# A four-layer graph network in split precision: products with high parts ahead of those with low parts at four waits, and the last output tile in two halves of columns

## What is computed

```
L0: attention over edges with 8 heads, Wo, layer norm,
    relu(h1 @ W1 + b1) @ W2 + b2 with 1024 hidden features, layer norm
L1: h @ wc + mean over edges of (h @ wn) + bias
L2: gates = softmax(h @ gate_W + gate_b), the best 2 of 4 experts;
    each expert twice: relu(mean_over_edges(h) @ Wl + bl + h @ Wr)
L3: H = X @ W + b, summed over edges and self loops with
    rsqrt(deg[src]) * rsqrt(deg[dst]), then relu
```

## Time and profile before

| | |
|---|---|
| median of 3 runs | 472.1 us (471.57 to 472.28) |
| the profiled execution, its own time | 472.32 us |
| its span in the trace | 470.3 us |
| TensorE's granted clock over the span | 0.996 of full speed |
| busy: TensorE products | 450.2 us, 96% |
| busy: TensorE weight loads (beside products) | 326.7 us, 69% |
| busy: VectorE, ScalarE, GpSimd | 310.4, 191.0 and 150.0 us |
| HBM read and written | 36.07 and 1.05 MB |

### The profile page before, as it was taken

The page is one execution under the profiler, slowest core; times in us unless marked ns, Lnnn a source line. Parts: engine busy times, 40 slices in busy tenths (PEclk is TensorE's granted clock), DMA queues, the critical chain, the costliest instruction groups (busy, mean ns, idle before and its releaser), DMA issues.

```text
span 470.3 us, 5919 instructions
## 1 busy us (share of the span) xinstructions
PE 450.2 (96%) x2096; PEld 326.7 (69%) x2096; DVE 310.4 (66%) x569; ACT 191.0 (41%) x266; POOL 150.0 (32%) x101
## 2 busy tenths in 40 slices
PE   8999999989899999799999999999999999999996
PEld 3456544434358888578778788888888888888765
DVE  5999868999997998953865836252263237134864
ACT  5898834537123440352632262133303332227230
POOL 4000033212112954454243444044434444344100
PEclk9999999989999999999999999999999999999999
DMA  8770007500000656145020222223221332020002
GB/s 275 160 294 1 1 2 168 101 0 0 1 1 1 149 144 200 24 79 191 1 64 27 91 89 91 89 89 113 90 91 32 115 144 77 14 89 1 0 1 89
DMA packets 24058, 37.48 MB, mean 80 GB/s; under 512 B 5728, under 2 KB 5984, under 8 KB 24032
## 3 DMA queue, kind: packets, MB, share of 16 engines
q1 hardware_dynamic: 21584, 32.80, 20.7%
q0 software_dynamic: 2160, 4.19, 5.2%
q10 hardware_dynamic: 288, 0.13, 0.1%
HBM read 36.07 MB, written 1.05 MB: 79 GB/s over the span
## 4 chain that ended last, share of the span: by engine, by line
PE 72%; DVE 16%; issue 5%; ACT 3%; POOL 2%; DVEq 1%; DMA 1%; POOLq 0%
PE ps L1240 16%; PE ps L1242 15%; PE ps L1241 15%; PE ps L1302 4%; PE ps L1313 4%; PE ps L1269 3%; PE ps L1268 3%; PE ps L1390 2%; DVE stats L762 2%; PE ps L1295 2%; DVE rsum L955 2%; DVE e_sb L395 1%; DVE one_src L836 1%; PE ps L1386 1%; PE ps L1412 1%
## 5 line engine op out<-in xcount | busy, mean ns | idle before, releaser
L473 POOL TENSOR_TENSOR w_lo<-w_stage,w_hi 128x1024 fp32r<-128x1024 f32 x21 | 51.6, 2456 | 136.4 <-ACT w_hi L559 125.7
L559 ACT ACTIVATE w_hi<-w_stage 128x2048 fp32r<-128x2048 f32 x22 | 42.0, 1909 | 53.4 <-PE ps L1242 53.4
L474 POOL TENSOR_TENSOR w_lo<-w_stage,w_hi 128x1024 fp32r<-128x1024 f32 x21 | 55.2, 2628 | 0.0
L1240 PE MATMUL ps<-w_hi,hid_hi 128*128 128x512 f32 x128 | 49.9, 390 | 0.5 <-DVE hid_lo L1151 0.5
L1242 PE MATMUL ps<-w_hi,hid_lo 128*128 128x512 f32 x128 | 49.8, 389 | 0.0
L1241 PE MATMUL ps<-w_lo,hid_hi 128*128 128x512 f32 x128 | 49.8, 389 | 0.0
L1240 PE MATMUL ps<-T_hi,w_hi 128*128 128x512 f32 (+1 forms) x112 | 41.0, 366 | 0.4 <-POOL w_lo L474 0.4
L1241 PE MATMUL ps<-T_lo,w_hi 128*128 128x512 f32 (+1 forms) x112 | 40.2, 359 | 0.0
L1242 PE MATMUL ps<-T_hi,w_lo 128*128 128x512 f32 (+1 forms) x112 | 40.2, 359 | 0.0
L1149 DVE TENSOR_SCALAR tmp<-ps,bl 128x512 f32<-128x512 f32 x16 | 12.0, 750 | 39.9 <-ACT hid_hi L713 39.9
L497 POOL TENSOR_TENSOR rstd<-vareps,scalars 128x1 f32<-128x1 f32 x24 | 15.9, 664 | 62.6 <-DVE vareps L764 62.6
(11 more groups left out here) (227 smaller groups left out, 984.4 us busy)
## 6 DMA issues: line engine op xcount, KB each, us to landing
w_stage<-in_L_gnn_Wr SPq DMA_DIRECT2D x8, 1024.0 KB, 5.3
w_stage<-in_L_gnn_Wl SPq DMA_DIRECT2D x8, 1024.0 KB, 5.0
w_stage<-in_L_gnn_W SPq DMA_DIRECT2D x5, 1024.0 KB, 5.7
x_sb<-in_x SPq DMA_DIRECT2D x4, 256.0 KB, 3.7
w_q<-in_L_gnn_Wq SPq DMA_DIRECT2D x1, 1024.0 KB, 7.8
w_k<-in_L_gnn_Wk SPq DMA_DIRECT2D x1, 1024.0 KB, 10.1
w_v<-in_L_gnn_Wv SPq DMA_DIRECT2D x1, 1024.0 KB, 5.7
w_o<-in_L_gnn_Wo SPq DMA_DIRECT2D x1, 1024.0 KB, 11.2
```

The lines of the kernel that those rows point to most:

```text
L473: gp.tensor_tensor(w_lo[h][:, 0:2], stage[s][:, 0:2], f32(w_hi[h][:, 0:2]), ALU.subtract)
L474: gp.tensor_tensor(w_lo[h][:, 2:4], stage[s][:, 2:4], f32(w_hi[h][:, 2:4]), ALU.subtract)\
L559: nc.scalar.activation(w_hi[home(u)][:], stage[u % 2][:], ACT.Copy).then_inc(hi_made, 1)
L1240: nc.tensor.matmul(goal, a_hi, b_hi, start=start, stop=False, **kw)
```

## The change

Five edits.

1. W1's second half: for its first bank, all eight products with high weights come first, after a wait for the high part alone (`hi_made`); then comes the wait for the low part and the four products with it.
2. Layer L2's mix over edges: in each step `k` the four products with `R4_hi` come first, after a wait for `hr_hi_made`, then the wait for `hr_lo_made` and the four with `R4_lo`.
3. Each expert's second layer: for `k` = 0 the eight products with `hid_hi` come first (after `hid_hi_made`), then the four with `hid_lo`. Other `k` are as before.
4. The last layer's mix: in steps 1 to 3 the four products with `R_hi` come ahead of the four with `R_lo`. On VectorE the low part of tile 1 is made ahead of `norm_shift` for tile 3.
5. The last output tile is computed in two halves of 256 columns. The left half stays in bank 7, the right half goes to bank 0. Each half has its own 12 products, its own two passes on VectorE and its own store. The start with `j` = 0 now covers three tiles only. Twelve products of 512 columns become 24 of 256.

```
+        def last_bank(t, half):
+            return 0 if half == 1 else 4 + t
...
-            for t in range(NT):
+            for t in range(NT - 1):
                 sp.wait_ge(x4_made, t + 1)
                 sp.dma_start(out[t * P:(t + 1) * P, :], x_sb[:, t, :]).then_inc(stored, 16)
-            sp.wait_ge(stored, 16 * NT)
+            for half in range(2):
+                sp.wait_ge(x4_made, NT + half)
+                cols = slice(half * HN, (half + 1) * HN)
+                sp.dma_start(out[(NT - 1) * P:NT * P, cols], x_sb[:, NT - 1, cols]).then_inc(stored, 16)
+            sp.wait_ge(stored, 16 * (NT + 1))
...
-            norm_shift(LN5, NT - 1)
-            for t in range(WHOLE, NT):
+            def last_row_lo(t):
                 v.wait_ge(last_hi_made, t - WHOLE + 1)
                 nc.vector.tensor_tensor(R_lo[:, t, :], h_sb[:, t, :], f32(R_hi[:, t, :]), ALU.subtract)\
                   .then_inc(last_lo_made, 1)
+            last_row_lo(WHOLE)
+            norm_shift(LN5, NT - 1)
+            for t in range(WHOLE + 1, NT):
+                last_row_lo(t)
...
+            def finish(n, t, cols=slice(0, D), half=None):
+                v.wait_ge(last_done, n)
+                v.wait_ge(bias_row_made, t + 1)
+                nc.vector.scalar_tensor_tensor(tmp[:, t, cols], ps[:, last_bank(t, half), cols], isd[:, t:t + 1],
+                                               tmp[:, t, cols], ALU.mult, ALU.add).then_inc(last_sum, 1)
+                v.wait_ge(last_sum, n)
+                v.wait_ge(nan_added, t + 1)
+                nc.vector.scalar_tensor_tensor(x_sb[:, t, cols], tmp[:, t, cols], 0.0, x_sb[:, t, cols], ALU.max,
+                                               ALU.add).then_inc(x4_made, 1)
...
+            for t in range(NT - 1):
+                finish(t + 1, t)
+            for half in range(2):
+                finish(NT + half, NT - 1, slice(half * HN, (half + 1) * HN), half)
...
-            hi, lo = weights(W1B)
-            for j in range(DT, FT):
+            hi, lo = w_hi[home(W1B)], w_lo[home(W1B)]
+            pe.wait_ge(hi_made, W1B + 1)
+            for k in range(DT):
+                nc.tensor.matmul(ps[:, DT, :], hi[:, k, col(0)], T_hi[:, k, :], start=k == 0, stop=False)
+                nc.tensor.matmul(ps[:, DT, :], hi[:, k, col(0)], T_lo[:, k, :], start=False, stop=False)
+            pe.wait_ge(lo_made, W1B + 1)
+            for k in range(DT):
+                last = nc.tensor.matmul(ps[:, DT, :], lo[:, k, col(0)], T_hi[:, k, :], start=False, stop=k == DT - 1)
+            last.then_inc(ff_done, 1)
+            for j in range(DT + 1, FT):
...
+                pe.wait_ge(hr_hi_made, k + 1)
+                for j in range(DT):
+                    nc.tensor.matmul(ps[:, 4 + j, :], R4_hi[:, k, col(j)], c_hi[:, k, :], start=k == 0, stop=False)
                 pe.wait_ge(hr_lo_made, k + 1)
                 for j in range(DT):
-                    goal = ps[:, 4 + j, :]
-                    nc.tensor.matmul(goal, R4_hi[:, k, col(j)], c_hi[:, k, :], start=k == 0, stop=False)
-                    last = nc.tensor.matmul(goal, R4_lo[:, k, col(j)], c_hi[:, k, :], start=False, stop=k == NT - 1)
+                    last = nc.tensor.matmul(ps[:, 4 + j, :], R4_lo[:, k, col(j)], c_hi[:, k, :], start=False,
+                                            stop=k == NT - 1)
...
-                for k in range(DT):
+                pe.wait_ge(hid_hi_made, DT * e + 1)
+                for t in range(NT):
+                    nc.tensor.matmul(ps[:, 4 + t, :], hid_hi[:, 0, col(t)], hi[:, 0, :], start=True, stop=False)
+                    nc.tensor.matmul(ps[:, 4 + t, :], hid_hi[:, 0, col(t)], lo[:, 0, :], start=False, stop=False)
+                pe.wait_ge(hid_lo_made, DT * e + 1)
+                for t in range(NT):
+                    nc.tensor.matmul(ps[:, 4 + t, :], hid_lo[:, 0, col(t)], hi[:, 0, :], start=False, stop=False)
+                for k in range(1, DT):
...
-                    pe.wait_ge(last_lo_made, k - WHOLE + 1)
+                    pe.wait_ge(last_hi_made, k - WHOLE + 1)
...
+                    else:
+                        nc.tensor.matmul(ps[:, j, :], R_hi[:, k, col(j)], loop_hi[:, k, :], start=False, stop=False)
+                if k >= WHOLE:
+                    pe.wait_ge(last_lo_made, k - WHOLE + 1)
+                    for j in range(DT):
+                        last = nc.tensor.matmul(ps[:, j, :], R_lo[:, k, col(j)], loop_hi[:, k, :], start=False,
+                                                stop=k == NT - 1)
+                        if k == NT - 1:
+                            last.then_inc(mix_done, 1)
...
-            for t in range(NT):
+            for t in range(NT - 1):
                 last_rows(t, 0)
-            for t in range(NT):
+            for t in range(NT - 1):
                 for j in range(1, DT):
                     last = last_rows(t, j)
+                last.then_inc(last_done, 1)
+            for half in range(2):
+                for j in range(DT):
+                    last = last_rows(NT - 1, j, half)
                 last.then_inc(last_done, 1)
```

More of the change, by code:

```diff
@@ L1622, in _ @@
                         last = mm3(ps[:, 4 + t, :], hid_hi[:, k, col(t)], hid_lo[:, k, col(t)], hi[:, k, :],
-                                   lo[:, k, :], k == 0, k == DT - 1)
+                                   lo[:, k, :], False, k == DT - 1)
                         if k == DT - 1:
@@ L1662, in _, with last_rows @@
                                          stop=False)
-                        continue
-                    nc.tensor.matmul(ps[:, j, :], R_hi[:, k, col(j)], loop_hi[:, k, :], start=False, stop=False)
-                    last = nc.tensor.matmul(ps[:, j, :], R_lo[:, k, col(j)], loop_hi[:, k, :], start=False,
-                                            stop=k == NT - 1)
-                    if k == NT - 1:
-                        last.then_inc(mix_done, 1)
+                    else:
[7 more added lines that the diff above has]
+                            last.then_inc(mix_done, 1)
             hi, lo = weights(W_LAST)
             pe.wait_ge(expert_sum, NT * EXPERTS)
-            def last_rows(t, j):
+            def last_rows(t, j, half=None):
                 pe.wait_ge(mix_lo_made, j + 1)
-                return mm3(ps[:, 4 + t, :], agg_hi[:, j, col(t)], agg_lo[:, j, col(t)], hi[:, j, :], lo[:, j, :],
-                           j == 0, j == DT - 1)
-            for t in range(NT):
+                n = slice(0, D) if half is None else slice(half * HN, (half + 1) * HN)
+                return mm3(ps[:, last_bank(t, half), n], agg_hi[:, j, col(t)], agg_lo[:, j, col(t)], hi[:, j, n],
+                           lo[:, j, n], j == 0, j == DT - 1)
+            for t in range(NT - 1):
                 last_rows(t, 0)
-            for t in range(NT):
+            for t in range(NT - 1):
                 for j in range(1, DT):
                     last = last_rows(t, j)
+                last.then_inc(last_done, 1)
+            for half in range(2):
+                for j in range(DT):
+                    last = last_rows(NT - 1, j, half)
                 last.then_inc(last_done, 1)
```

8 lines of the change are left out of this document (removed).

## The result

| | before | changed |
|---|---|---|
| median, 6 runs each | 471.84 us (471.45 to 472.28) | 468.25 us (468.03 to 469.24) |
| ratio | | 0.9926, 95% interval 0.9916 to 0.9935 |
| profiled execution: own time / span | 472.32 / 470.3 us | 468.27 / 466.5 us |

The change makes the kernel 3.6 us faster. In the profile of the changed kernel each place of the sum can be read for itself.

What follows compares the result with a forecast made beforehand. TensorE, at 96% of the span, was taken as the bound, so only its waits and the tail could give time. Terms summed to 3.29 us: 472.32 to 469.0, said as 469.1 for possible leaks, range 468.4 to 470.9.

Steps and rivals of the forecast that it cites:

- W1: First tile of W1's second half: the 0.57 us gap and the 0.10 restart go, -0.67 us, passed on to later stages.
- L2's mix: Layer L2's mix over edges: four steps without a wait, 2.29 us each, end at 237.07 instead of 238.02, -0.95 us.
- first expert: Second weights of the first expert: the 0.65 us gap and 0.10 restart go, -0.75 us; nothing at the other three.
- last mix: Last layer's mix: 1.03 us won, 0.68 lost again waiting for bank 0, which finishes fifth of eight: -0.35 us.
- Halves: Last output tile in two halves: +0.16 us for TensorE's 24 shorter products, -0.53 us for VectorE's two shorter passes.
- Last transfer: Final store of 128 KB instead of 256 KB: -0.2 us, taken between bounds of nothing and 1.0.
- covers that may leak: Times by which low parts are ready before TensorE wants them, thinnest 0.14 us; four terms use them, so 469.1 was said.
- 1: Rival: at the touched waits only the idle time in brackets comes back, 1.83 us in all, giving 470.5; chance 0.19.
- 2: Rival: W1's 0.67 us is lost in the normalisations behind it, set by VectorE's own queue, giving 469.8; chance 0.09.
- 3 (a held subtraction): Rival: GpSimd's weight split holds VectorE's subtraction for the first expert's second low part; TensorE stands 3.9 us, 472.9; chance 0.03.
- 4: Rival: no change, the waits come back elsewhere on TensorE, under 0.2% (0.94 us) is left, giving 471.8; chance 0.06.
- a new draw: VectorE and GpSimd share a port pair that one instruction holds whole, so every shift of timing redraws which subtractions are held.

## Why the prediction was right, and where not

- **W1, L2's mix, first expert, last mix**: 0.67, 0.95, 0.75 and 0.35 were forecast, 0.67, 0.96, 0.79 and 0.36 measured. The way each edit was costed, a stream of products at their own pace to the point where the next engine takes over, and not the idle time in brackets, is what the runs bear out. That the last mix gives 0.68 of its 1.03 back through bank 0's place is shown by putting the place back. One reading was loose: the 0.84 of idle time on VectorE, taken as its room behind W1, stands in front of the second of the normalisations' rows; the room in front of the first was 0.81, and 0.36 of it is left.
- **Halves**: +0.16 and -0.53 to the digit.
- **Last transfer**, the term that was mis-sized: "I take -0.2, near the lower bound". What lies behind VectorE's last row fell by 0.33. In the span it fell by 0.14: the last store lands 1.87 us after its issue on average in the eight profiles with halves, and after 2.01 with whole tiles. So size does count for little, as the prediction said, and this part is near the forecast. The other 0.19 lies outside the span, stays when the last store is whole again or late, and so isn't the transfer's; the sum had no term for it.
- **The base**, the step that put the time outside the range: "472.32 - 3.29 = 469.0; from the median it would be 468.8. Four of the terms use up covers that may leak a little, so I say 469.1". The profiled execution of the kernel before held a half-clock stretch that cost 0.55 us, which the 3-us windows above show (0.89 and 0.55 at 96 to 102 us), and it lay 0.25 above the mean of its kernel and 0.48 above the median of the six runs beside the changed kernel. From the mean, 472.07 less 3.48 (the sum as measured) is 468.6, from the median of the six runs 468.4. Both are within 0.2 us of the measured mean and median, 468.43 and 468.25, less than single executions scatter. So the 0.85 between 469.1 and 468.25 are 0.48 of the base, 0.19 of terms, 0.13 of it the one called last transfer, 0.07 of rounding up for covers that might leak, of which none did, and 0.11 that stay open. The range's lower end was worked out from a better transfer alone, 469.0 - 0.6; from the median of 472.1, which the prediction names too, the same working gives 468.2 and holds the result. The scatter of the kernel before, 0.8 us over six runs, should have gone into the range on both sides.
- **Rivals**: 1 and 2 fell to the runs above; 3 (a held subtraction) and 4 didn't occur in any of the profiles of the changed code. Nor was a shift of timing "a new draw": in all sixteen profiles the same five subtractions into a low part take longer than 1.2 us, each as long within 0.02 us as in the kernel before, the longest 5.42 or 5.43 at W1's result, though they start up to 2.5 us earlier.

## What to carry to other kernels

Cost a removed wait as a stream of products at their own pace up to the next engine's turn, and ask in the same breath which bank the next reader needs first: an order that puts all high parts first also finishes every bank late. Before a profile is made the base of a sum, look for stretches of lower clock in it and compare its own time with the other runs; where a fall has a price and a chance, it belongs in the range. And a store in two parts gains by the early start of the first: two halves issued together were 0.9 us slower here.

## What the hardware showed beyond expectation

- TensorE's clock fell to half for some 3 us behind an idle time of about 2 us, at two places, in some executions and not in others; it cost 0.5 to 0.7 us at one and 0.1 at most at the other. Idle times of 1.3 us and less in the same stages were never followed by it in the profiles. With 1.06 us of repeated products in the first idle time it was absent at both places in three of three profiles, though the second idle time was as long as ever.
- The clock over the span was 1.0 in 5 of 11 executions of the kernel with W1's edit alone, and in 1 of 33 of the kernel before beside it. But the other kernels that hold this edit, without repeated products, have 1.0 in 2 of 35, so it isn't shown that the edit moves the odds.
- A low part that is ready 0.05 us before TensorE wants it still makes the product behind it last 0.50 us instead of 0.39.
- The time outside the span fell from 2.01 to 1.80 us in all kernels whose last tile is computed in halves, whatever their stores. With it, a transfer of 8 KB on queue q14 moved from behind the span's end into the last store's time.
